# Pairs of batches in loops per window for 24 tiles, and the list of further pairs ahead of the next chunk, in a graph network on one Trainium2 core

## What is computed

```python
xj = x[src] @ g
gauss = jnp.exp(jnp.sum(-0.5 * diff * diff / (EPS + sigma[None] ** 2), axis=-1))
msg = jnp.einsum('eko,ek->eo', xj.reshape(E, K, OUT_DIM), gauss)
summed = segment_sum(msg, dst); aggr = summed / max(cnt, 1)
x = layernorm(x + silu(aggr + x @ root_w + bias + x))
h = relu(sage(x, W_self1, W_neigh1, b1)); y = sage(h, W_self2, W_neigh2, b2)
# sage(h) = h @ W_self + (segment_sum(h[src], dst) / max(deg, 1)) @ W_neigh + b
return layernorm(x + y)
```

## Time and profile before

| | |
|---|---|
| median of 3 runs | 8670.53 us (8668.92 to 8673.6) |
| the profiled execution | 8678.05 us, its span 8676.2 us |
| TensorE busy | 5695.0 us, 66% of the span |
| VectorE busy | 5445.3 us, 63% |
| ScalarE busy | 3649.4 us, 42% |
| GpSimd busy | 3304.5 us, 38% |
| chain that ended last | PE 40%, DVE 26%, issue 15%, DVEq 11%, ACT 6% |

### The profile page before, as it was taken

How to read it: one execution, slowest core, us unless ns; L and a number is a source line. 1 busy time by engine, 2 the same in 40 slices (tenths; PEclk the granted TensorE clock), 3 DMA queues, 4 the chain that set the end, 5 groups by cost and what they waited for, 6 DMA issues and landing times.

```text
span 8676.2 us, 164515 instructions
## 1 busy us (share of the span) xinstructions
PE 5695.0 (66%) x36739; PEld 4139.9 (48%) x36740; DVE 5445.3 (63%) x19820; ACT 3649.4 (42%) x11389; POOL 3304.5 (38%) x3146
## 2 busy tenths in 40 slices
PE   2554444454566666666666666666665579999999
PEld 2211212122233444444444444444443579999999
DVE  4765656666777887887788787777775132222222
ACT  3211313233466776766666666666663100000000
POOL 4111212233456666666666666666660000000000
PEclk6555656666777888888888888888886589999999
DMA  3000101111122322222222222222221079999998
GB/s 85 6 20 20 39 21 39 38 42 43 61 78 81 98 83 88 92 82 82 85 92 82 82 81 81 92 76 79 82 75 56 13 284 380 382 381 371 386 384 349
DMA packets 268131, 1082.97 MB, mean 125 GB/s; under 512 B 152902, under 2 KB 153926, under 8 KB 204102
## 3 DMA queue, kind: packets, MB, share of 16 engines
q1 hardware_dynamic: 152502, 968.66, 28.7%
q0 software_dynamic: 100352, 102.96, 6.7%
q10 hardware_dynamic: 14902, 8.11, 0.4%
HBM read 751.67 MB, written 327.81 MB: 124 GB/s over the span
## 4 chain that ended last, share of the span: by engine, by line
PE 40%; DVE 26%; issue 15%; DVEq 11%; ACT 6%; DMA 1%; SPq 0%; ACTq 0%
PE pw L797 18%; DVE rE L1040 12%; PE pw L693 9%; DVE rE L1039 9%; PE pw L671 6%; ACT rE L508 4%; PE pw L705 4%; DVEq L1116 2%; DVEq L1057 2%; DVEq L1039 2%; PE pw L768 1%; ACT rB L538 1%; DVE rE L1084 1%; DVEq L1122 1%; DVE local L1078 1%
## 5 line engine op out<-in xcount | busy, mean ns | idle before, releaser
L464 POOL DMA_INDIRECT rE<-in_x,idx x3136 | 3302.4, 1053 | 3199.6 <-DMA idx<-idx_d 2137.1
L1040 DVE TENSOR_SCALAR rE<-iperm,gcol,wbase 128x392 f16<-128x392 f16 x7504 | 2858.3, 381 | 0.0
L538 ACT CAST rB<-pw 128x792 bf16<-128x792 f32 x1568 | 1249.6, 812 | 2936.7 <-PE pw L705 2935.9
L1039 DVE TENSOR_SCALAR rE<-iota_h,locol 128x128 f16<-128x128 f16 x7568 | 2145.2, 283 | 525.6 <-issue 418.8
L705 PE MATMUL pw<-rE 128*128 128x396 f16 x6272 | 1566.3, 382 | 1342.2 <-DVE rE L1040 1066.0
L508 ACT ACTIVATE rE<-rE,cols 128x64 f32<-128x64 f32 x9408 | 2330.7, 337 | 8.9 <-DMA tab<-tab_d 8.9
L693 PE MATMUL pw<-rE 128*128 128x193 f32 x7824 | 1720.1, 382 | 386.0 <-DVE rA L1036 341.3
L693 PEld LDWEIGHTS pw<-rE 128*128 128x128 f32 x7824 | 1577.6, 227 | 590.6 <-DVE rE L1084 552.1
L705 PEld LDWEIGHTS pw<-rE 128*128 128x128 f16 x6272 | 573.4, 104 | 2217.8 <-issue 1202.3
L671 PE MATMUL pw<-rE 128*128 128x396 f16 x1296 | 579.9, 483 | 552.8 <-DVE rE L1040 550.5
L797 PE MATMUL pw<-rB,rA 128*128 128x192 bf16 x9604 | 810.0, 246 | 6.5 <-DMA rA<-count 6.5
(11 more groups left out here) (205 smaller groups left out, 1738.3 us busy)
## 6 DMA issues: line engine op xcount, KB each, us to landing
rA<-count SPq DMA_DIRECT2D x392, 1568.0 KB, 8.4
count<-rB SPq DMA_DIRECT2D x98, 3136.0 KB, 10.0
rE<-in_x,idx POOLq DMA_INDIRECT x3136, 2.5
cols<-cols_d SPq DMA_DIRECT2D x98, 64.0 KB
cols_d<-rA SPq DMA_DIRECT2D x3, 1568.0 KB, 5.2
rA<-in_edge_attr ACTq DMA_DIRECT2D x1, 4608.0 KB
out<-gcol ACTq DMA_DIRECT2D x97, 32.0 KB, 5.9
rE<-in_x SPq DMA_DIRECT2D x24, 128.0 KB, 2.2
```

What stands on the lines that cost most here:

```text
L464: pool.indirect_dma_start(out=gath[:, s, u * CB + b, :], out_offset=None, in_=x, in_offset=bass.IndirectOffsetOnAxis(ap=idx[:, s, u * CB + ...
L538: act.copy(stage[:, s, :, j * 2 * W:(j + 1) * 2 * W].rearrange("p h (w n) -> p w h n", w=2), pw[j % 2][:, :, 0:CW].rearrange("p w (h n) -> ...
L1039: V.tensor_scalar(left, iota_h[:], locol[:, bass.ds(b, 1)], None, ALU.is_equal)
L1040: return V.tensor_scalar(right[:, 0:GW], iperm[:], gcol[:, bass.ds(b, 1)], base, ALU.subtract, ALU.is_equal)
```

## The change

For the first DT = 24 tiles, `first_tile` takes the place of `tile_counts` on VectorE and TensorE. Each of the 32 windows is a loop over all its pairs, whose number and first batch are in one word of the window. The 32 words stand in the table where the list stood (a second copy into `tabw`), and `many_w`, 16 registers, is loaded twice a tile on each of the two engines, ahead of units 0 and 8 (L1144 on VectorE, L727 on TensorE in the changed kernel). The one-hots have a ring of 2 RU = 8 slots of one window, chosen by a counter of pairs modulo 8 in a register; VectorE waits in each turn for `x_used` of the slot (L1082), TensorE for `x_rdy`. TensorE starts each window's bank with a matmul with zeros (L665) and ends a unit with another (L734). These tiles have no list and no add into `stage`.

For the other 74 tiles the list, still at least one entry, stands ahead of the table load and of chunk 0 of the next tile, on VectorE and on TensorE. It uses slots 4 to 7 of the ring, so VectorE waits first until TensorE is through with the tile's last unit (L1179, before the loop of pairs); `xlo` and `xcomp` are gone. The one-hots of a batch are written from `ones_of` (L1071 and L1073 of the changed kernel), with the same two instructions. The diff, cut to the lines that do this:

```diff
-            def rest(many):
-                pe.wait_ge(x_add, pe.snap(xk, min_val=1, max_val=1 << 24))
-                pe.matmul(pb[5][:, 0:1], zero[:, 0:P], zero[:, 0:1], start=True, stop=False, skip_group_check=True)
+            def pairs(bank, many, slot, before):
+                ins = pe.matmul(bank[:, 0:1], zero[:, 0:P], zero[:, 0:1], start=True, stop=False, skip_group_check=True)
+                if before is not None:
+                    ins.then_inc(before, 1)
                 with pe.Fori(0, many, 1):
                     q = pe.snap(xr, min_val=1, max_val=1 << 24)
-                    for h in range(2):
-                        pe.wait_ge(x_rdy, q + h)
-                        pe.matmul(pb[5][:, 0:CW], xlo[:, h, :], xcomp[:, h, :], start=False, stop=False,
-                                  skip_group_check=True).then_inc(x_used, 1)
-                    pe.reg_add(xr, xr, 2)
+                    r = slot(q)
+                    pe.wait_ge(x_rdy, q)
+                    for b in range(2):
+                        ins = pe.matmul(bank[:, 0:CW], lo1h[:, bass.ds(r, 1), b, :].rearrange("p o c -> p (o c)"),
+                                        comp[:, bass.ds(r, 1), b, :].rearrange("p o c -> p (o c)"), start=False, stop=False,
+                                        skip_group_check=True)
+                    ins.then_inc(x_used, 1)
+                    pe.reg_add(xr, xr, 1)
+            def rest(many):
+                pe.wait_ge(x_add, pe.snap(xk, min_val=1, max_val=1 << 24))
+                pairs(pb[5], many, lambda q: q % RU + RU, None)
                 pe.reg_add(xk, xk, 1)
...
+            def first_tile(t, s):
+                for u in range(U):
+                    if u:
+                        chunk(t, s, u)
+                    if u % 2 == 0:
+                        pe.load(many_w, tab[0:1, s, T_X + u // 2 * LW:T_X + (u // 2 + 1) * LW])
+                    for n in range(u * NU // U, (u + 1) * NU // U):
+                        pe.wait_ge(a_evac, t * NU + (n + 1))
+                        pe.sem_inc(s_tick[0], 1)
+                        for w in range(2):
+                            pairs(pw[n % 2][:, w, :], part_of(many_w[(2 * n + w) % LW], 1, PK, NB // 2), lambda q: q % (2 * RU),
+                                  a_chunk if n % (NU // U) == 0 and w == 0 else None)
+                        pe.matmul(pw[n % 2][:, 1, 0:1], zero[:, 0:P], zero[:, 0:1], start=False, stop=False,
+                                  skip_group_check=True).then_inc(a_used, 1)
+                chunk(t + 1, 1 - s, 0)
...
-                pe.reg_mov(extra, words[0])
-                if not last:
-                    chunk(t + 1, 1 - s, 0)
-                with pe.Fori(0, pe.snap(extra, min_val=1, max_val=JW), 1) as e:
+                with pe.Fori(0, pe.snap(words[0], min_val=1, max_val=JW), 1) as e:
                     pe.load([xw], tab[0:1, s, bass.ds(e * 2 + T_X, 1)])
                     v = pe.snap(xw, min_val=JW, max_val=(1 << 24) - 1)
                     rest(pe.snap(v // JW, min_val=1, max_val=NB // 2))
+                if not last:
+                    chunk(t + 1, 1 - s, 0)
...
-            with pe.Fori(0, NT // 2 - 1, 1) as i:
+            with pe.Fori(0, DT // 2, 1) as i:
                 for s in range(2):
-                    tile_counts(i * 2 + s, s, False)
+                    first_tile(i * 2 + s, s)
+            with pe.Fori(0, (NT - DT) // 2 - 1, 1) as i:
+                for s in range(2):
+                    tile_counts(i * 2 + (s + DT), s, False)
...
+            link(V.tensor_copy(tabw[0:NT], tabf[0:NT]))
+            V.tensor_copy(tabw[0:DT, T_X:T_X + JW], winw[0:DT]).then_inc(s_tabw, 1)
...
-            def ones_of(left, right, b, base):
-                V.tensor_scalar(left, iota_h[:], locol[:, bass.ds(b, 1)], None, ALU.is_equal)
-                return V.tensor_scalar(right[:, 0:GW], iperm[:], gcol[:, bass.ds(b, 1)], base, ALU.subtract, ALU.is_equal)
-            def rest_of(b0, many, base):
+            def ones_of(r, b, base):
+                one = isinstance(r, int)
+                for h in range(2):
+                    V.tensor_scalar(lo1h[:, r, h, :] if one else lo1h[:, bass.ds(r, 1), h, :].rearrange("p o c -> p (o c)"),
+                                    iota_h[:], locol[:, bass.ds(b + h, 1)], None, ALU.is_equal)
+                    ins = V.tensor_scalar(comp[:, r, h, 0:GW] if one else
+                                          comp[:, bass.ds(r, 1), h, 0:GW].rearrange("p o c -> p (o c)"),
+                                          iperm[:], gcol[:, bass.ds(b + h, 1)], base, ALU.subtract, ALU.is_equal)
+                return ins
+            def pairs_of(b0, many, base, free, slot):
                 with dve.Fori(0, many, 1) as c:
                     q = dve.snap(xr, min_val=1, max_val=1 << 24)
+                    r = slot(q)
+                    dve.wait_ge(x_used, q + free)
                     b = nc.s_assert_within(b0 + c * 2, 0, NB, skip_runtime_bounds_check_because="b0 + 2 many <= NB + 1")
-                    for h in range(2):
-                        dve.wait_ge(x_used, q + h)
-                        ones_of(xlo[:, h, :], xcomp[:, h, :], b + h, base).then_inc(x_rdy, 1)
...
-                    dve.reg_add(xr, xr, 2)
-                dve.wait_ge(x_used, dve.snap(xr, min_val=1, max_val=1 << 24) + 1)
+                    ones_of(r, b, base).then_inc(x_rdy, 1)
+                    dve.reg_add(xr, xr, 1)
+            def rest_of(b0, many, base):
+                pairs_of(b0, many, base, RU, lambda q: q % RU + RU)
+                dve.wait_ge(x_used, dve.snap(xr, min_val=1, max_val=1 << 24) + (2 * RU - 1))
...
+            def first_tile(i, s):
+                t = i * 2 + s
+                base_of(t, s)
+                for u in range(U):
+                    if u % 2 == 0:
+                        dve.load(many_w, tab[0:1, s, T_X + u // 2 * LW:T_X + (u // 2 + 1) * LW])
+                    for n in range(u * NU // U, (u + 1) * NU // U):
+                        for w in range(2):
+                            word = many_w[(2 * n + w) % LW]
+                            pairs_of(part_of(word, 0, PK, 0, NB - 2), part_of(word, 1, PK, 1, NB // 2),
+                                     wbase[:, s, 2 * n + w:2 * n + w + 1], 0, lambda q: q % (2 * RU))
+                    if u < U - 1:
+                        prepare(i, s, u + 1)
+                    elif s == 0:
+                        prepare(i, 1, 0)
+                    else:
+                        prepare(i + 1, 0, 0)
+                dve.wait_ge(a_evac, t * NU + (NU + 2))
+                dve.sem_inc(s_tick[3], 1)
+                bound_of(t, s)
...
-                dve.reg_mov(extra, words[T_XT])
+                with dve.Fori(0, dve.snap(words[T_XT], min_val=1, max_val=JW), 1) as e:
+                    dve.load(xw, tab[0:1, s, bass.ds(e * 2 + T_X, 2)])
+                    v = dve.snap(xw[0], min_val=JW, max_val=(1 << 24) - 1)
+                    j = dve.snap(v % JW, min_val=0, max_val=JW - 1)
+                    b0, many = dve.snap(xw[1], min_val=0, max_val=NB), dve.snap(v // JW, min_val=1, max_val=NB // 2)
+                    dve.wait_ge(a_used, t * NU + (NU + RU))
+                    dve.sem_inc(s_tick[3], 1)
+                    rest_of(b0, many, wbase[:, s, bass.ds(j, 1)])
+                    dve.wait_ge(a_evac, t * NU + (NU + 2))
+                    counts = stage[:, s, :, bass.ds(j * W, W)]
+                    V.tensor_tensor(counts, pb[5][:, 0:CW].rearrange("p (h n) -> p h n", n=W), counts, ALU.add).then_inc(x_add, 1)
+                    dve.reg_add(xk, xk, 1)
                 if s == 0:
                     prepare(i, 1, 0)
                 elif not last:
                     prepare(i + 1, 0, 0)
-                dve.wait_ge(a_evac, 2 * NU * i + (s * NU + NU + 2))
-                dve.sem_inc(s_tick[3], 1)
-                with dve.Fori(0, dve.snap(extra, min_val=1, max_val=JW), 1) as e:
-                    dve.load(xw, tab[0:1, s, bass.ds(e * 2 + T_X, 2)])
-                    v = dve.snap(xw[0], min_val=JW, max_val=(1 << 24) - 1)
-                    j = dve.snap(v % JW, min_val=0, max_val=JW - 1)
-                    rest_of(dve.snap(xw[1], min_val=0, max_val=NB), dve.snap(v // JW, min_val=1, max_val=NB // 2),
-                            wbase[:, s, bass.ds(j, 1)])
-                    counts = stage[:, s, :, bass.ds(j * W, W)]
-                    V.tensor_tensor(counts, pb[5][:, 0:CW].rearrange("p (h n) -> p h n", n=W), counts, ALU.add).then_inc(x_add, 1)
-                    dve.reg_add(xk, xk, 1)
                 dve.wait_ge(x_add, dve.snap(xk, min_val=1, max_val=1 << 24))
-                V.tensor_reduce(bound[:, bass.ds(i * 2 + s, 1)] if not isinstance(i, int) else bound[:, 2 * i + s:2 * i + s + 1],
-                                stage[:, s, NT, :], AX_X, ALU.max).then_inc(a_bnd, 1)
+                bound_of(t, s)
...
-            with dve.Fori(0, NT // 2 - 1, 1) as i:
```

(12 more changed lines are left out.)

45 lines of the change are left out of this document (22 added, 23 removed).

## The result

The changed kernel takes 8719.02 us (8710.04 to 8725.04), the kernel before 8673.6 beside it (8668.92 to 8677.36): ratio 1.0051, interval 1.0036 to 1.0066. Run again on another chip it gave 8720.28 us and 1.0057 (1.004 to 1.0074). So it is slower by 45 us, where 85 us less had been forecast. Two chips used for some of the experiments ran the kernel before 2170 and 2350 us longer than the others did, and the kernels of the experiments that ran on both kinds of chip 2090 to 2730 us longer; totals from there are not used, only single records and loops that show the same in all.

The account below looks back on a forecast made before the run. VectorE's own stream was taken to bound the count stage. 194 us gained in the first 24 tiles less 109 lost in the other 74 gave 85 gained, 8585 us from the median of 8670.5; range 8400 to 8760.

Parts of the forecast that it names:

- The turn: New window loops, first 24 tiles: 1.39 us a turn on VectorE, set by its sequencer; 1.44 for a loop's first turn.
- 24 x 46.1 + 748: First 24 tiles: 46.1 us a tile for 32 first turns at 1.44, plus 538 further turns at 1.39, 748 us.
- Rival 1: New loops: the vector unit, not the sequencer, is the pace; turns near 1.15 us, about 8270 us; chance 0.14.
- rival 3: New loops: a turn costs more than 1.45 us, so slower; 8795 us at 1.55, 8860 at 1.60; chance 0.18.
- Rival 4: New loops: some jumps back are far ones at 2.9 to 5.8 us, 100 to 200 us, 8685 to 8785; chance 0.06.
- The fixed part of a loop tile: First 24 tiles, beside the one-hots: 19.3 us a tile for tile start, chunk steps, table load, new loads and jump.
- I take the dear one, 3.7 each, 7.4 per tile: First 24 tiles: two new 16-word loads a tile at 3.7 us each; the other end was 1.3 each, 115 us less.
- The chunk steps: First 24 tiles: four a tile at 1.5 us, 6.0 in all, plus some 30 us for six tiles with a fifth.
- the 2348 of the forecast: Forecast length of the first 24 tiles in us with the new loops, against 2542 before: 194 us gained.
- The other 74 tiles: Tile ends, list moved ahead of the table load: 0.6 us lost in 47 tiles, 3.0 in 27; 109 us lost.
- 6.7 later and 3.1 back: Tile ends with two chunk steps: everything from the table load on 6.7 us later, 3.1 us won back at the end.
- Rival 2: Other 74 tiles: the moved list costs nothing, most of 109 us less lost, about 8490 us; chance 0.12.

Follow-up runs that it names:

- half-width run: The changed kernel with the second one-hot of the loops made for 196 of 392 columns, so half of the counts are left out: 8754.68 us.
- delayed write: The changed kernel with SyncE's write of a tile's counts waiting until TensorE is through with the next tile's first unit: 8609.94 us, 0.9937 of before.
- aligned one: The changed kernel with the table padded to 96 words, so every long load starts at a multiple of 16 words: 8401.59 us, 0.9694 of before.
- list-behind one: The changed kernel with the list of the 74 tiles again behind the table load and chunk step: 8610.77 us, 0.9935 of before.

## Why the forecast was wrong, point by point

**The turn** was right, with the sequencer as its pace: forecast were 1.39 us and 1.44 for a window's first turn, measured 1.35 and 1.39 (medians; means 1.37 and 1.43, since 99 turns are some 0.4 us longer, which was not followed). The turns stand in 96 stretches with nothing between them. From a stretch's first one-hot to the start of its last they sum to 1762 us, and that last one-hot takes 0.39: 1800 for 1306 turns, where the forecast had 24 x 46.1 + 748 = 1854. 54 us less. Rival 1 (vector unit as pace) is out by the half-width run, rival 3 (over 1.45) by the timeline, though the time came out on its side. That 8719 lies between the forecast's 8400 and 8760 is luck: it is there as a loss, by a term for which no rival stood. Rival 4 is out too: from the branch to the next record of the sequencer no turn of the 1306 shows over 0.43 us.

**The fixed part of a loop tile** is the step that failed: "I take the dear one, 3.7 each, 7.4 per tile". The range named for it, 1.3 to 3.7, came from loads at moments without a large transfer. The new place of the load, right behind L1129, is the moment in a tile when SyncE's write of 3136 KB out of the SBUF starts. Forecast 178 us for 48 loads, measured 293 (the 24 first 206, the 24 second 87): 115 more, of which the delayed write gives back 119. No row of before had a long load at that moment: L1065 stands ahead of the write.

**The chunk steps** were taken at 1.5 us from a row that stops at TensorE's first matmul. The second half of the one-hots (L1084, now L1123), the way out of the loop and the first turn's registers lie behind it. Measured 222 us for 102 steps (2.2 each) against 174: 48 more. Together +115 + 48 - 54 is 109 of the 112 us by which 2460 exceeds the 2348 of the forecast; the other 3 lie in the table loads, tile starts and jumps.

**The other 74 tiles**: the mechanism was right, VectorE waiting for TensorE's last unit with the table load queued behind; forecast 109, measured 124. The ends with one step lost 1.25 us (0.6 forecast), with two 3.41 (3.0 forecast; the forecast's own terms, 6.7 later and 3.1 back, give 3.6, and it took 3.0 without saying why): 121 us by the order where 109 stood, and 27 by the new loop of pairs, a term that the forecast did not have, less what came back inside the tiles. Rival 2 is out.

So 194 should have been 82 and 109 should have been 124: 85 us of gain became 42 of loss in the profiles and 45 in the medians. The chances for slower add up to 0.28 (0.04, 0.18 and 0.06) and not to 0.27; nothing hangs on it.

The forecast's sentence on the Trainium skill, "DMA: Bandwidth & Descriptors", Latency and other measured facts, and "Runtime: NRT & Kernel Launch", Instruction fetch mechanics, gave a floor of about 600 ns and, at about 200 ns a register, an estimated 3.2 us for 16 words. By the section Terms of "Runtime: NRT & Kernel Launch" in the Trainium skill such loads fetch registers from HBM, while the table here lies in the SBUF, so the figure need not carry over. The trace has 3.62 us from words 23, 39, 110 and 126; from multiples of 16 words it has 1.10, or 69 ns a register, which that rule does not give. A load of two words takes 0.53 us, a little under the floor. At the jumps back of the two-tile loop the runs show 2.1 to 3.3 us, as means of a stage, and nothing like it in the loops of pairs (rival 4).

## What to carry to other kernels

A loop with addresses in registers costs what its register records cost; count them first, since they, and not the vector work, may be its pace. Price a new load or wait at the place where it will stand: look what the other queues do at that moment, and if a large transfer starts there, move one of the two. Words that a sequencer loads in bulk should start at a round place in their table (here a multiple of 16 words); that alone took 3.6% off the changed kernel, 8719 to 8402 us, and put it 3.1% below the kernel before.

## What the runs showed of the hardware

- A load of words into registers depends on where it starts: 21 words 1.60 us from word 0 or 96, 4.7 from word 87; 16 words 1.10 from words 32, 48, 128 and 144, 3.62 from 23, 39, 110 and 126.
- While the write of 3136 KB from SBUF runs, the same 16 words take 8.0 to 9.4 us from words 23 and 110, and 3.7 to 3.8 from word 32.
- The jump back of the two-tile loop cost VectorE 2.2 us on average in the last 74 tiles of the changed kernel, 3.3 in the half-width and in the aligned one, 2.8 in the list-behind one and before.
- Halving the free size of an f16 compare, 392 to 196 columns, took its record from 0.38 to 0.33 us only.
- On the two chips on which all kernels took longer, VectorE's sequencer showed stretches of up to some 20 records of 0.7 us each where the others have 0.05 to 0.2, for example (a profile of the half-width kernel there):

```profile
L1081 DVEq MOVE  x2: 708/716/725, 2382.2 to 2392.7; - x2
L1098 DVEq FUSED_REGOPS  x2: 690/694/699, 2380.8 to 2391.3; - x2
```

What causes these stretches stayed open.
